# A two-layer recurrent block on one core: narrow products in place of transposes, one wait, the end and one setup product moved

## The reference

```
xn = layernorm(x)
x  = x + attention0(xn) * silu(ternary_mlp(xn))          # layer 0, one head of 128, hidden 512
xn = layernorm(x)
s  = layernorm(recurrent(xn)) * ln_scale + ln_bias       # layer 1
g  = silu(attention16(xn) + mixture_of_8_experts(xn))
out = x + s * g
```

## Time and profile before

| | |
|---|---|
| Median of 3 runs | 1012.39 us (1012.34 to 1013.4) |
| Profiled execution | 1012.52 us, span 1010.7 us |
| PE busy | 960.6 us (95%), 6930 products |
| ACT busy | 746.0 us (74%) |
| DVE busy | 547.9 us (54%) |
| POOL busy | 198.5 us (20%) |
| Moved by transfers | 22.18 MB |

### The profile page before, as it was taken

One profiled execution on the slowest core, in us unless ns is written; L12 is line 12 of the kernel. 1 busy time (PEld: TensorE's weight loads), 2 busy tenths in 40 slices (PEclk: granted clock), 3 DMA queues, 4 the chain that ended last, 5 costly groups with the idle time before them and its releaser, 6 DMA issues.

```text
span 1010.7 us, 17808 instructions
## 1 busy us (share of the span) xinstructions
PE 960.6 (95%) x6930; PEld 536.1 (53%) x6930; DVE 547.9 (54%) x1336; ACT 746.0 (74%) x914; POOL 198.5 (20%) x145
## 2 busy tenths in 40 slices
PE   3999999999899999999989999999999999999995
PEld 2888633343488853334358874334437886333431
DVE  6655735645556654554565574456447556346262
ACT  5543699989763479998956359998985446999885
POOL 1200202412300020441130020233212002035023
PEclk9999999999999999999999999999999999999998
DMA  6000133000000023200000012310000002320000
GB/s 249 1 1 1 24 48 62 1 3 1 1 22 1 2 39 50 43 2 2 1 22 1 1 17 43 51 24 2 2 1 22 1 1 26 51 35 2 2 1 23
DMA packets 17625, 22.18 MB, mean 22 GB/s; under 512 B 2976, under 2 KB 14336, under 8 KB 17280
## 3 DMA queue, kind: packets, MB, share of 16 engines
q1 hardware_dynamic: 17536, 20.99, 10.3%
HBM read 7.85 MB, written 2.10 MB: 10 GB/s over the span
## 4 chain that ended last, share of the span: by engine, by line
PE 76%; DVE 8%; ACT 7%; issue 6%; POOL 2%; DMA 0%; POOLq 0%; DVEq 0%; ACTq 0%
PE ps L1105 73%; ACT big L1064 3%; PE ps L1527 2%; DVE st L279 1%; ACT xn L1036 1%; DVE wk L563 1%; DVE wk L739 1%; ACT spl L1017 1%; ACT qz L1012 1%; DVE flags L420 1%; PE ps L1125 1%; DVE xn L452 1%; POOL st L877 1%; PE ps L1520 0%; DVE spl L460 0%
## 5 line engine op out<-in xcount | busy, mean ns | idle before, releaser
L1064 ACT ACTIVATE big<-ps 128x1024 f32<-128x1024 f32 x512 | 493.6, 1034 | 40.2 <-PE ps L1105 38.2
L1105 PE MATMUL ps<-big,vaug 128*32 128x512 f32 x2048 | 272.6, 604 | 3.6 <-DVE wk L739 2.3
L1105 PE MATMUL ps<-hid 32*128 32x512 f32 x1024 | 130.5, 493 | 4.3 <-ACT big L1064 2.9
L1105 PE MATMUL ps<-hid,fw_sb 128*128 128x512 f32 x416 | 101.2, 397 | 0.3 <-DVE hid L468 0.3
L980 ACT ACTIVATE wk<-ps,cols_sb 128x512 f32<-128x512 f32 x64 | 40.6, 687 | 80.2 <-PE ps L1105 74.4
L877 POOL TENSOR_TENSOR st<-st 128x4 f32<-128x4 f32 x16 | 16.2, 1010 | 389.0 <-DVE st L552 287.5
L1105 PEld LDWEIGHTS ps<-hid 32*128 32x128 f32 x1024 | 49.3, 181 | 81.5 <-issue 50.6
L891 POOL TENSOR_TENSOR qz<-qz,wk 128x512 f32<-128x512 f32 x32 | 41.2, 1288 | 244.0 <-DVE wk L709 244.0
L1105 PEld LDWEIGHTS ps<-hid,fw_sb 128*128 128x128 f32 x416 | 77.5, 188 | 18.5 <-DVE hid L468 1.1
L1105 PEld LDWEIGHTS ps<-big,vaug 128*32 128x32 f32 x2048 | 41.0, 108 | 69.6 <-issue 35.2
L727 DVE SCALAR_TENSOR_TENSOR big<-ps,sm,big 128x128 f32<-128x128 f32 x128 | 44.3, 346 | 47.0 <-PE ps L1105 35.8
(11 more groups left out here) (215 smaller groups left out, 1577.8 us busy)
## 6 DMA issues: line engine op xcount, KB each, us to landing
hid<-spl SPq DMA_DIRECT2D x288, 32.0 KB
xnext<-in_x SPq DMA_DIRECT2D x4, 512.0 KB, 4.0
out<-qz SPq DMA_DIRECT2D x8, 256.0 KB, 2.3
big<-in_fw SPq DMA_DIRECT2D x1, 1877.0 KB, 9.3
hid<-one_row SPq DMA_DIRECT2D x16, 96.0 KB
wk<-in_lw SPq DMA_DIRECT2D x1, 1476.0 KB, 14.2
big<-in_fw SPq DMA_DIRECT2D x1, 939.0 KB, 11.1
cst_sb<-in_cst SPq DMA_DIRECT2D x1, 440.0 KB, 4.4
```

What stands on the lines that cost most here:

```text
L1064: up(ms_exp, a.activation(prob[:, at:at + 2 * CH].rearrange("p (h n) -> p h n", n=CH), ps[:, bank:bank + 2, :], ACT.Exp, scale=HDM ** -0.5))
L1105: return t_.matmul(out_, lhsT, rhs, start=start, stop=stop, **kw)
```

## The change

The diff does five things:

1. `nat`: the four transposes become 16 products. Each has 32 columns of `oT` as the stationary operand, writes 32 partitions, and moves 36 columns of the identity (4 heads x 9). The result lies packed, 9 columns a head instead of 32.
2. `ht`: the same with 8 moving columns (4 x 2).
3. The sixth q,k unit (i = 5) waits for 4 instead of 5 of `prod_ok`.
4. In the last batch GpSimd does only the first half of the end. DVE does the second half in two quarters of 256 columns, with semaphores of their own; ACT makes the Silu of the quarters, and SP stores them one by one.
5. In the first batch the flags' product and the Wo product come behind the u products, row scores 2 to 5 behind these, and the comparison's result is loaded only then.

```diff
-                    if t % 2 == 1:
+                    if t % 2 == 1 and b:
                         row_scores(2 + t // 2)
...
+                if b == 0:
+                    t_.wait_ge(setup_v, marks["flags"])
+                    mm(ps[:, 1, 0:1], ones, flags[:, 0:1], True, True).then_inc(setup_p, 1)
+                    t_.wait_ge(setup_v, marks["half Wo"])
+                    for m in range(KM):
+                        ins = mm(ps[:, 0, 0:D], ones, wo_sb[:, m * D:(m + 1) * D], m == 0, m == KM - 1)
+                    ins.then_inc(setup_p, 1)
+                    for t in range(2, 6):
+                        row_scores(t)
+                    t_.wait_ge(wide_ok, 1)
+                    mm(ps[:, 1, 0:1], ones, flags[:, 0:1], True, True)
+                    wide = t_.value_load(iflag[0:1, 0:1], min_val=0, max_val=1)
...
-                        t_.wait_ge(prod_ok.sem, prod_ok.at(b, i))
+                        t_.wait_ge(prod_ok.sem, prod_ok.at(b, 4 if i == 5 else i))
...
+                        needed = ident.rearrange("p (m r) -> p m r", r=QUAD)[:, :, 0:P // HD1]
                         for q in range(TPC):
-                            ins = t_.transpose(side[:, q * P:(q + 1) * P], xn[:, (i * TPC + q) * P:(i * TPC + q + 1) * P], ident)
+                            for g in range(GH):
+                                at = (i * TPC + q) * P + QUAD * g
+                                ins = mm(ps[QUAD * g:QUAD * (g + 1), SIDE_BANK, q * H1:(q + 1) * H1], xn[:, at:at + QUAD], needed, True, True)
...
+                        needed = ident.rearrange("p (h r) -> p h r", r=QUAD)[:, :, 0:HDM + 1]
                         for q in range(TPC):
-                            ins = t_.transpose(ps[:, bank, q * P:(q + 1) * P], oT[i % 2][:, q * P:(q + 1) * P], ident)
+                            for g in range(GH):
+                                at = q * P + QUAD * g
+                                ins = mm(ps[QUAD * g:QUAD * (g + 1), bank, q * GH * (HDM + 1):(q + 1) * GH * (HDM + 1)],
+                                         oT[i % 2][:, at:at + QUAD], needed, True, True)
```

The end, on DVE (behind the loop over the batches) and on ACT (in the last batch):

```diff
+            v.wait_ge(msum_ok.sem, msum_ok.at(b, 1))
+            v.wait_ge(att_ok.sem, att_ok.at(b, 2 * NG))
+            for h in range(2):
+                tl = slice(TPC + 2 * h, TPC + 2 * h + 2)
+                v.tensor_tensor(att[:, tl, :], att[:, tl, :], moe[:, tl, :], ALU.add).then_inc(end_sum, 1)
+            v.wait_ge(o_done.sem, o_done.at(b, 1))
+            for h in range(2):
+                tl = slice(TPC + 2 * h, TPC + 2 * h + 2)
+                v.wait_ge(end_g2, h + 1)
+                v.tensor_tensor(g2[:, tl, :], g2[:, tl, :], xnv[:, tl, :], ALU.mult).then_inc(end_sg, 1)
+                v.wait_ge(end_sg, h + 1)
+                v.tensor_tensor(fin[:, tl, :], g2[:, tl, :], xres[:, tl, :], ALU.add).then_inc(end_fin, 1)
...
+                if b == B - 1:
+                    a.wait_ge(sum_ok[0].sem, sum_ok[0].at(b, 1))
+                    up(g2_ok, a.activation(qz[:, 0, 0:CH], big[:, 1, 2, 0:CH], ACT.Silu))
+                    for h in range(2):
+                        a.wait_ge(end_sum, h + 1)
+                        sl = slice(CH + 2 * P * h, CH + 2 * P * (h + 1))
+                        a.activation(qz[:, 0, sl], big[:, 1, 2, sl], ACT.Silu).then_inc(end_g2, 1)
+                    break
```

More of the change, by code:

```diff
@@ L262, in build_program @@
         ex_mm, ex_ok, msum_ok = sig("ex_mm", 2 * NT), sig("ex_ok", 2 * NT), sig("msum_ok", 1, 1)
-        g2_ok, fin_ok = sig("g2_ok", 2), sig("fin_ok", 2, 1)
-        stored = sig("stored", 32, 1)
+        g2_ok, fin_ok = sig("g2_ok", 2, 0, 1), sig("fin_ok", 2, 1, 1)
+        stored = sig("stored", 32, 1, 16)
+        end_sum, end_g2, end_sg, end_fin, end_stored = (sem(n_) for n_ in ("end_sum", "end_g2", "end_sg", "end_fin", "end_stored"))
         def col(name, k=0):
@@ L360, in _ @@
                     up(x_in, load_x(b + 1), 16)
+                o = out[bass.ds(b, 1)].rearrange("o (t p) d -> p (o t) d", p=P)
                 for c in range(NCH):
+                    if c and b == B - 1:
+                        break
                     sp.wait_ge(fin_ok.sem, fin_ok.at(b, c + 1))
-                    o = out[bass.ds(b, 1)].rearrange("o (t p) d -> p (o t) d", p=P)
                     up(stored, sp.dma_start(o[:, c * TPC:(c + 1) * TPC, :], fin[:, c * TPC:(c + 1) * TPC, :]), 16)
             sp.wait_ge(x_in.sem, x_in.at(B, 0))
-            sp.wait_ge(stored.sem, stored.at(B, 0))
+            for h in range(2):
+                sp.wait_ge(end_fin, h + 1)
+                tl = slice(TPC + 2 * h, TPC + 2 * h + 2)
+                sp.dma_start(o[:, tl, :], fin[:, tl, :]).then_inc(end_stored, 16)
+            sp.wait_ge(stored.sem, stored.at(B, 0) - 16)
+            sp.wait_ge(end_stored, 32)
         @block.vector
@@ L744, in attention_out @@
                     v.wait_ge(oN_mm.sem, oN_mm.at(b, n_ + 1))
-                    oN = ps[:, NAT_LAST_BANK if n_ == 2 * NG - 1 else SIDE_BANK, :].rearrange("p (i n) -> p i n", n=QUAD)
+                    oN = ps[:, NAT_LAST_BANK if n_ == 2 * NG - 1 else SIDE_BANK, 0:TPC * GH * (HDM + 1)].rearrange("p (i n) -> p i n", n=HDM + 1)
                     step(v.reciprocal(rec, oN[:, :, HDM]))
@@ L909, in _ @@
                 g_.wait_ge(msum_ok.sem, msum_ok.at(b, 1))
-                for c in range(NCH):
+                halves = range(NCH) if b < B - 1 else range(1)
+                for c in halves:
                     tl = slice(c * TPC, (c + 1) * TPC)
@@ L1143, in _ @@
                 split3(ps[:, c, :], gh_hi[:, 0:D], gh_lo[:, 0:D], xt_hi[:, sl], xt_lo[:, sl]).then_inc(r_mm.sem, 1)
[L1144 to L1148, removed]
             attended = ExitStack()
```

14 lines of the change are left out of this document (5 added, 9 removed).

## The result

The changed kernel takes 1001.59 us (median of 5, 999.73 to 1002.21) against 1012.64 (median of 5, 1012.34 to 1013.4): a ratio of 0.9885 (95% interval 0.9871 to 0.9900), 11 us faster. The forecast was 996.0, in a range of 992 to 1006; the measured time lies in this range, but outside the 993 to 999 that the forecast kept for itself, and beside the 1001 of rival C. The profiled execution is the fastest of the five: 999.73, with a span of 997.9, so its trace shows 12.8 us less than the trace of before; the median has only 11.

The account below looks back on a forecast made before the run. The prediction took TensorE (PE) as the bound, busy 95% of the span and leading 76% of the wait chain. Pieces 10.1, q,k unit 2.8, end 3.6 and setup 0 made 16.5 off 1012.5: 996.0 us, range 992 to 1006.

Parts of the forecast that it names:

- rival C: Attention loops: ACT or DVE takes half of the attention's gain, giving 1001; chance 0.12.
- The round, 0.033: TensorE's `nat` pieces: each round of four column groups costs 0.033 us, bound by moving columns; a cycle gains 0.33.
- 0.027 for `ht`: TensorE's `ht` pieces, 8 moving columns: a round costs 0.027 us, as four passes still have to be issued.
- Full gain where a `nat` stands alone: Attention cycles 11, 19, 35, 43, 51, 59, PE-bound: 0.33 us each, less 0.02 in the last four.
- The last `nat`: A batch's last `nat` piece, behind a wait for its copy: gains 0.15 us per batch.
- The sixth q,k unit: First cycle of batches 2 to 4: waiting for four products starts it 0.93 us earlier, 2.8 in three batches.
- The end, 3.6: Last batch's end split between POOL and DVE: saves 3.6 us, lower bound 2.6; last store 3.8 earlier.
- The setup, 0: Batch 1's start, flag's product behind row scores: net 0 us, bounds -0.5 to +1.0.
- Six of these take 1.18 at first and 0.62 later: Batch 1's u products on TensorE: half clock, 1.2 GHz, for some 4.5 us after PE begins.
- A: TensorE's pieces: a round costs 0.11 us whatever it moves, giving 1012.8; chance 0.10.
- B: TensorE's pieces: instructions aren't supplied fast enough, a piece cycle takes about 3.1 us, giving 1038; chance 0.07.
- D: Outside attention: an edit there gives nothing, the end above all, giving 999.6; chance 0.05.

Follow-up runs that it names:

- b_end_new: Changed kernel with another end: GpSimd adds 96 columns early, VectorE operands in PSUM, one store, VectorE's jump before its last heads' copy; 1000.27 us, ratio 0.9870.
- d_best: Changed kernel with another order in batch 1's start, b_end_new's end, and TensorE's jump to its last block before the last heads' product; 999.78 us.

## Why the prediction was right, and where its sizes were off

The mechanism was right, the interval (11 us) lies well clear of the 2 us that count as no change, and every part moved the way it was put down. The sum of 16.5 was 3.7 too large against the profiled execution and 5.5 against the median. So the hit rests on the wide range and not on the sum; the missing gain brought the time to rival C's 1001, but not by C's way, for the loops kept 8.0 of their 9.5.

- **The round, 0.033.** Right for `nat` (0.0325); its path was right too. 0.027 for `ht` was too low (0.031): something other than the moving columns sets that round, either the 32 stationary columns or the issue of four passes. A `nat` cycle gained 0.285, not 0.33, since the last four passes are spread (0.282 from first to last instead of 0.25) and scores follow 0.13 behind them. Over all `nat` cycles that is 0.9 us, with the 0.02 that the forecast had taken off four of them.
- **"Full gain where a `nat` stands alone"**, cycle 27 nothing, 8 and 9 at 0.30 and 0.18: measured 0 and 0.28 and 0.18. What took gain away beyond that was not ACT, on which the part was spent, but VectorE's copy-out in cycle 10: 0.57 in four batches, a wait that the forecast did not have. The last `nat` gave nothing instead of 0.6.
- **The sixth q,k unit.** 0.93 forecast, 0.91 measured, in all three batches.
- **The end, 3.6.** 2.3. The steps were counted right; two durations were wrong, both by a neighbour: a VectorE sum beside POOL's addition, which made the last addition 0.8 late, and a store beside instruction loads, 0.8 late too. The 3.8 forecast for the last store less these is 2.2. The first was to be had from the rows: the earlier trace rows time POOL's additions with VectorE idle, and the forecast ran both engines at once without asking what they share. The Trainium skill, SBUF — State Buffer, section SBUF: two separate sides, says that VectorE reading two inputs from SBUF and a GpSimd operation that reads SBUF share a pair of ports: the one that starts first has it for its whole instruction, and the other blocks. The trace agrees: 0.43 became 1.49 and ended 0.28 behind GpSimd's addition, and 0.75 for two products with an operand in PSUM did not stretch. By that the end would have been put at an estimated 2.8.
- **The setup, 0.** Right in the profiled execution (0.1), and within its bounds of -0.5 to +1.0 in most, but the bounds missed the one of 3.4. The 0.1 is in part luck: the forecast had the clock low to 25.5 and high after it, and the trace has it high from 18.5 to 22.0 and low from there to 32.2. "Six of these take 1.18 at first and 0.62 later" was read as a fixed time from TensorE's start, and the traces have no such fixed time.

Rivals A and B are ruled out by the starts of the rounds and by the 0.28 of a whole piece; C and D each hold a part: C's loss came from another wait, D's end gave two thirds.

## What to carry to other kernels

Where a small product's result is wanted in few columns, count both operands: narrow the moving one, and group the stationary one in the same grouping as the neighbours; stop where a narrower one no longer shortens the round. When work moves to an idle engine, look what runs beside it then, not what ran beside it before, and which operands both read from SBUF. And at the start of a kernel look when TensorE's products become fast: with one and the same order of work that came between 30.4 and 40.1 us, so one trace does not tell what an order costs.

## What the runs showed of the hardware

- A taken jump costs more than its own time: in the changed kernel VectorE jumps at 993.98, and its next instruction comes 2.96 later; TensorE's jump at 989.88 has a record of 3.75 (3.51 in the kernel before). Loads of 16 and 8 KB follow them over a DMA engine that stores use too; a store then landed 0.8 and 2.1 us late (the changed kernel, b_end_new), its last packets coming one at a time as if from a single engine. The Trainium skill, Runtime: NRT & Kernel Launch, section Instruction fetch mechanics, says that a jump out of the loaded pages forces a load of 16 KB blocks before work goes on; the traces agree (d_best, 2.65 between two passes with a load of 16 KB among them), and add what it does to transfers beside it.
- The loop is exact: over nine profiled executions with the same pieces a batch's loop (138 to 139 us) agrees within 0.3, while in the nine with the same new order of work the last row maximum ends anywhere from 37.9 to 41.5. Of this kernel's spread, that is what traces show; the executions 3 to 4 us above their medians were not profiled with the faster orders.
- Fp32 passes of four groups of 32 start 7 ns apart within a round, and a round comes every 32 ns: 32 passes in 0.28 us. Rounds of two groups of 64 come every 58 ns, single passes of 128 every 112.
